# Splitting node rows on two engines: VectorE makes the remainders and third parts, GpSimd only rounds; a small pair of steps in the edge loop goes to ScalarE

## The reference

```python
N, E, IN, H, D, EF = 6250, 100000, 256, 8, 32, 3
x1 = layernorm(x)                                   # rows of 256
h  = (x1 @ W.T).reshape(N, H, D)
alpha = (h[src] * a_src).sum(-1) + (h[dst] * a_dst).sum(-1) \
      + (relu(edge_attr @ edge_W.T + edge_b).reshape(-1, H, D) * h[dst]).sum(-1)
alpha = where(alpha >= 0, alpha, 0.2 * alpha)
ex    = exp(alpha - segment_max(alpha, dst)[dst])   # softmax over the edges of a target
attn  = ex / maximum(segment_sum(ex, dst)[dst], 1e-10)
x = x + segment_sum(h[src] * attn[..., None], dst) + bias
x = x + top2_of_8_experts(layernorm(x))             # LN, 256 -> 1024, gelu, 1024 -> 256
```

## Time and profile before

| what | value |
|---|---|
| median of 3 runs | 2120.4 us (2117.72 to 2121.09) |
| the profiled execution's own time | 2123.07 us |
| its span, first to last instruction | 2121.2 us |
| mean granted TensorE clock | 0.963 |
| busy over the span | PE 91%, DVE 73%, ACT 59%, POOL 59% |
| first stage | up to about 116.5 us of the span |
| edge stage | from there to about 1200 us |

### The profile page before, as it was taken

One profiled execution on the slowest core, in us unless ns is written; L12 is line 12 of the kernel. 1 busy time (PEld: TensorE's weight loads), 2 busy tenths in 40 slices (PEclk: granted clock), 3 DMA queues, 4 the chain that ended last, 5 costly groups with the idle time before them and its releaser, 6 DMA issues. The chain is left out here.

```text
span 2121.2 us, 45176 instructions
## 1 busy us (share of the span) xinstructions
PE 1928.2 (91%) x12492; PEld 1499.8 (71%) x12492; DVE 1542.0 (73%) x3518; ACT 1260.7 (59%) x3557; POOL 1248.5 (59%) x1149
## 2 busy tenths in 40 slices
PE   7559899999999999999999666899999999999997
PEld 5426566666666666666666334899999999999996
DVE  7749899999999999999999887544444444444442
ACT  3438788888888888888888565433333333333332
POOL 5777777777777776666665000355555555555553
PEclk9769999999999999999999877999999999999998
DMA  9355555555555555555444596122222222222221
GB/s 250 108 155 156 153 151 156 156 153 154 152 158 149 148 150 142 150 143 143 141 136 120 208 346 130 48 36 36 41 36 36 40 37 36 38 38 36 38 39 23
DMA packets 161229, 242.11 MB, mean 114 GB/s; under 512 B 36895, under 2 KB 115519, under 8 KB 160866
## 3 DMA queue, kind: packets, MB, share of 16 engines
q0 software_dynamic: 61920, 139.45, 27.6%
q1 hardware_dynamic: 90362, 92.12, 14.7%
q10 hardware_dynamic: 8712, 7.65, 1.1%
HBM read 202.22 MB, written 36.91 MB: 113 GB/s over the span
## 5 line engine op out<-in xcount | busy, mean ns | idle before, releaser
L717 POOL DMA_INDIRECT arena<-h_tab,src x784 | 752.9, 960 | 291.1 <-issue 201.7
L1737 ACT ACTIVATE arena<-psum,arena 128x128 f32<-128x128 f32 x840 | 239.5, 368 | 519.0 <-PE psum L1687 519.0
L919 PE MATMUL psum<-arena 128*128 128x264 f32 x1760 | 475.1, 393 | 1.4 <-DVE arena L1016 1.4
L1687 PEld LDWEIGHTS psum<-arena 128*128 128x128 f32 x3360 | 393.1, 193 | 7.7 <-issue 2.4
L1687 PE MATMUL psum<-arena 128*128 128x128 f32 x3360 | 393.7, 276 | 2.0 <-DVE arena L1759 2.0
L898 PE MATMUL psum<-arena 128*128 128x256 bf16 x2640 | 376.3, 278 | 17.6 <-DVE arena L993 17.5
L1703 PE MATMUL psum<-arena 128*128 x1680 | 379.8, 379 | 0.0
L1649 POOL DMA_INDIRECT out_rows<-arena,src x105 | 212.5, 2024 | 250.4 <-DVE arena L1772 247.5
L919 PEld LDWEIGHTS psum<-arena 128*128 128x128 f32 x1760 | 299.6, 190 | 83.7 <-issue 47.9
L898 PEld LDWEIGHTS psum<-arena 128*128 x2640 | 246.1, 98 | 133.2 <-issue 69.6
L1703 PEld LDWEIGHTS psum<-arena 128*128 128x128 f32 x1680 | 311.1, 190 | 38.0
(11 more groups left out here) (241 smaller groups left out, 1965.2 us busy)
## 6 DMA issues: line engine op xcount, KB each, us to landing
arena<-rel_list SPq DMA_DIRECT2D x110, 256.0 KB
arena<-h_tab,src POOLq DMA_INDIRECT x784
arena<-ea_slots SPq DMA_DIRECT2D x440, 27.0 KB
arena<-in_x SPq DMA_DIRECT2D x12, 896.0 KB, 12.8
arena<-in_W SPq DMA_DIRECT2D x16, 512.0 KB, 8.2
arena<-in_W SPq DMA_DIRECT2D x8, 1024.0 KB, 12.2
h_tab<-arena SPq DMA_DIRECT2D x6, 952.0 KB, 7.9
out_rows<-arena SPq DMA_DIRECT2D x5, 896.0 KB, 12.0
```

What stands on the lines that cost most here:

```text
L717: pool.indirect_dma_start(rows[:, (p % RING * U + k) * TW:(p % RING * U + k + 1) * TW], None, d.h_tab[:, :], bass.IndirectOffsetOnAxis(ap= ...
L919: last = nc.tensor.matmul(ps[:, AGG + a % 2, 0:HS], oh[:, a % OH, k, :], msg[:, a % MSG, k, :], start=(k == 0), stop=(k == U - 1))
L1687: last = nc.tensor.matmul(ps[:, UP + 2 * b + h // 4, h % 4 * P:(h % 4 + 1) * P], w_now[:, b, m, h * P:(h + 1) * P], xT[:, b, m * P:(m + 1) ...
L1737: last = nc.scalar.activation(hT[:, b, h * P:(h + 1) * P], ps[:, UP + 2 * b + half, h % 4 * P:(h % 4 + 1) * P], ACT.Gelu, bias=b1_now[:, b ...
```

## The change

In the first stage GpSimd keeps the two roundings of a group; the two subtractions go to VectorE as `without_first_part` and `last_part`, counted by a new semaphore `left`. VectorE's list gets them at hand-chosen places: three between the statistics of groups 4 and 5, one behind those of group 6, eight among the edge attributes. There is a fourth place for node rows, which lies over the last two lists of `pieces` (edge attributes), so ACT's rounding of attribute list 2 has to wait until group 3 has left that place. `STAGE_OF` says which group uses which place, and ACT waits for group i-4 instead of i-3. The turn of the target list on PE and ACT comes one group later (`REL_AT`).

In the edge stage `fall` is made by ScalarE, with the sign turned (Relu of new minus old maximum, and the exponential of its negative), and `scale` too.

```diff
+STAGE_OF = (1, 2, 0, 3, 1, 2, 0)
@@ prepare
+        late_pieces = c.arena[:, lists.at - 2 * PW:lists.at]
+        c.stage.append(late_pieces[:, 0:GT * TW])
-        REL_AT = 3
+        REL_AT = 4
@@ GpSimd
             for i in range(GROUPS - 1):
                 pool.wait_ge(h_copied, (i + 1) * GT + 2)
                 nc.gpsimd.tensor_copy(first, h).then_inc(cast, 1)
-                pool.wait_ge(cast, 4 * i + 1)
-                nc.gpsimd.tensor_tensor(rest, h, first, ALU.subtract).then_inc(cast, 1)
-                pool.wait_ge(cast, 4 * i + 2)
+                pool.wait_ge(left, 2 * i + 1)
                 nc.gpsimd.tensor_copy(second, rest).then_inc(cast, 1)
-                pool.wait_ge(cast, 4 * i + 3)
-                nc.gpsimd.tensor_tensor(third, rest, second, ALU.subtract).then_inc(cast, 1)
-                pool.wait_ge(cast, 4 * i + 4)
@@ ScalarE, take_h
-                    if i >= 3:
-                        act.wait_ge(rows_stored[i - 3], 32)
-                        act.wait_ge(cast, 4 * (i - 3) + 2)
+                    if i >= 4:
+                        act.wait_ge(rows_stored[i - 4], 32)
+                        act.wait_ge(left, 2 * (i - 4) + 1)
@@ ScalarE, first_part
+                if g == 2:
+                    act.wait_ge(rows_stored[3], 32)
+                    act.wait_ge(left, 7)
@@ VectorE
+            def without_first_part(i):
+                h, rest, first, _, _ = parts_of(c, i)
+                dve.wait_ge(cast, 2 * i + 1)
+                if i:
+                    dve.wait_ge(left, 2 * i)
+                nc.vector.tensor_tensor(rest, h, first, ALU.subtract).then_inc(left, 1)
+
+            def last_part(i):
+                _, rest, _, second, third = parts_of(c, i)
+                dve.wait_ge(cast, 2 * i + 2)
+                dve.wait_ge(left, 2 * i + 1)
+                nc.vector.tensor_tensor(third, rest, second, ALU.subtract).then_inc(left, 1)
...
@@ edges, ScalarE
             def factor(ch):
+                before = c_fwd[:, 1 - ch % 2, 2 * CT - 1:2 * CT]
+                act.wait_ge(chain_scanned, 2 * ch + 2)
...
+                nc.scalar.activation(fall, before, ACT.Relu, bias=c_top[:, 0:1], scale=-1.0).then_inc(fall_made, 1)
                 act.wait_ge(fall_made, ch + 1)
-                nc.scalar.activation(fall, fall, ACT.Exp).then_inc(factor_made, 1)
+                nc.scalar.activation(fall, fall, ACT.Exp, scale=-1.0).then_inc(factor_made, 1)
...
+            def node_scale(ch):
+                act.wait_ge(factored, ch + 1)
+                act.wait_ge(first_kept, 2 * ch + 2)
+                if ch > 1:
+                    act.wait_ge(rescaled, ch - 1)
+                nc.scalar.activation(scale, ps[:, SM, 0:H], ACT.Identity, scale=first[:, ch % 4:ch % 4 + 1], bias=others[:, ch % 4:ch % 4 + 1]).then_inc(scale_made, 1)
@@ edges, VectorE
-                nc.vector.tensor_scalar(fall, before, c_top[:, 0:1], 0.0, ALU.subtract, ALU.min).then_inc(fall_made, 1)
...
-                nc.vector.tensor_scalar(scale, ps[:, SM, 0:H], first[:, ch % 4:ch % 4 + 1], others[:, ch % 4:ch % 4 + 1], ALU.mult, ALU.add).then_inc(scale_made, 1)
```

More of the change, by code:

```diff
@@ L116, in parts_of @@
 def parts_of(c, i):
-    h = c.stage[i % 3].rearrange("p (k h f) -> p k h f", h=H, f=FW)[:, :, :, 1:D + 1]
+    h = c.stage[STAGE_OF[i]].rearrange("p (k h f) -> p k h f", h=H, f=FW)[:, :, :, 1:D + 1]
     rest = c.arena[:, LISTS:LISTS + REST_WORDS].rearrange("p (k h f) -> p k h f", k=GT, h=H)
@@ L145, in prepare @@
          xT_made, xT_copied, h_made, h_copied, zeros_stored, lists_gathered, tiles_gathered, rel_made, turned,
-         turned_back, derived, links_made, ends_same, cut, rests, cast) = semaphores(
+         turned_back, derived, links_made, ends_same, cut, rests, cast, left) = semaphores(
             nc, ctx, "p_consts", "p_zeros", "p_w", "p_small", "p_hi", "p_himade", "p_val", "p_below", "p_counted",
@@ L238, in _ @@
             for i in range(GROUPS - 1):
-                h, rest, first, second, third = parts_of(c, i)
+                h, rest, first, second, _ = parts_of(c, i)
                 pool.wait_ge(h_copied, (i + 1) * GT + 2)
                 nc.gpsimd.tensor_copy(first, h).then_inc(cast, 1)
-                pool.wait_ge(cast, 4 * i + 1)
-                nc.gpsimd.tensor_tensor(rest, h, first, ALU.subtract).then_inc(cast, 1)
-                pool.wait_ge(cast, 4 * i + 2)
+                pool.wait_ge(left, 2 * i + 1)
                 nc.gpsimd.tensor_copy(second, rest).then_inc(cast, 1)
-                pool.wait_ge(cast, 4 * i + 3)
-                nc.gpsimd.tensor_tensor(third, rest, second, ALU.subtract).then_inc(cast, 1)
-                pool.wait_ge(cast, 4 * i + 4)
         @block.sync
@@ L276, in tables @@
                 sp.dma_start(d.h_tab[(i * GT + k0) * P:(i * GT + k1) * P, :].rearrange("(k p) n -> p k n", p=P),
[L277 removed]
+                             c.stage[STAGE_OF[i]][:, k0 * TW:k1 * TW].rearrange("p (k n) -> p k n", k=k1 - k0)).then_inc(rows_stored[i], 16)
             def attributes(g):
@@ L484, in _ @@
             nc.vector.memset(c.stage[0].rearrange("p (n f) -> p n f", f=FW)[:, :, 0], 1.0).then_inc(zeros_made, 1)
+            nc.vector.memset(c.stage[3].rearrange("p (n f) -> p n f", f=FW)[:, :, 0], 1.0).then_inc(zeros_made, 1)
             nc.vector.memset(two_stages.rearrange("p (n f) -> p n f", f=FW)[:, :, 0], 1.0).then_inc(zeros_made, 1)
@@ L607, in _ @@
             group(4)
+            without_first_part(0)
+            last_part(0)
+            without_first_part(1)
             deviations(3)
@@ L615, in _ @@
             split_weights()
-            for g in range(SG):
-                without_first(g)
-                third_part(g)
+            without_first(0)
+            without_first_part(2)
+            third_part(0)
+            last_part(2)
+            without_first_part(3)
+            without_first(1)
+            last_part(3)
+            third_part(1)
+            without_first_part(4)
+            without_first(2)
+            last_part(4)
+            third_part(2)
+            without_first(3)
+            without_first_part(5)
+            third_part(3)
+            last_part(5)
+            dve.wait_ge(left, 2 * (GROUPS - 1))
             dve.wait_ge(ends_same, 3)
@@ L1128, in _ @@
                     shift(ch)
-                for ch in due(t, 8):
-                    node_scale(ch)
                 if t % CS in AHEAD_OF and SELECTED * 2 <= t + AHEAD_OF[t % CS] < SLOTS:
```

18 lines of the change are left out of this document (9 added, 9 removed).

## The result

The changed kernel takes 2094.9 us (median of 4 runs, 2094.0 to 2096.4) against 2120.7 us before (4 runs, 2117.7 to 2128.6): ratio 0.9879, 95% interval 0.9856 to 0.9902. 2097 was forecast. The profiled execution took 2095.04 us, with a span of 2093.2 us, 28.0 us less than before.

What follows compares the result with a forecast made beforehand. First stage bound by GpSimd's splitting; edge stage by gathers until about 400 us, then VectorE and TensorE together. 17.9 + 5.6 = 23.5 us off 2123.07 gives 2099.6, less 2.7 for the median: 2097 us, range 2085 to 2110.

Steps and rivals of the forecast that it cites:

- the term of the edges: Edge stage: two operations leaving VectorE gain 0.14 us in each of 40 chunks, 5.6 us.
- the stage: First stage: subtractions moved to VectorE let the first gather start at 99.6 instead of 117.47, gaining 17.9 us.
- four meetings: First stage: VectorE and GpSimd instructions excluding each other on the shared port, four times 1.7 us.
- ScalarE's new wait ahead of attribute list 2: First stage: waiting until group 3's store landed and it left its place costs nothing, covered by an earlier wait.
- The two long waits: ScalarE, first stage: 7.27 us for a store would go; 18.10 us for the first attribute remainder would end 19.2 earlier.
- All of it goes through: First stage to end: as gathers pace the first 15 chunks, the whole 17.9 us reaches the final time.
- the cut down to 0.14: Edge stage, L1054: of its 0.20 us a chunk only 0.14 pays, ScalarE's side being ready at 413.68, VectorE's at 413.62.
- rival 2: Edge stage: 0.40 us a chunk pays in full because ScalarE's run moves with the faster chunk; 2086 us, chance 0.13.
- The chain as the bound: First stage: handing groups between VectorE and GpSimd bounds it; gain 9 there, 5 in the edges, 2106 us, chance 0.20.
- The edges paying in full: Edge stage: all 0.40 us a chunk taken off VectorE arrives, 16 us; total 2086 us, chance 0.13.
- ScalarE as the bound: Edge stage: ScalarE's added 0.5 us a chunk delays TensorE, up to 28 us lost against 18 gained; 2130, chance 0.05.
- Nothing was swallowed: Denies the rival that late gathers or early chunks no faster than TensorE's start-up swallow the gain; 2118, chance 0.06.

Runs made afterwards that it cites:

- experiment 8: Changed kernel with a small register edit, three row places instead of four, the split kept on two engines; ratio 0.9919 to the kernel before, on a slower chip.
- experiment 7: Changed kernel with a small register edit, both subtractions back on GpSimd, four row places kept; ratio 0.9990 to the kernel before, on a slower chip.
- experiments 1 and 2: 1: changed kernel with wait registers taken modulo 512, 2097.6 us. 2: that kernel with the old edge stage, so the new first stage alone, 2109.7 us.
- experiments 3 and 4: Changed kernel with a small register edit, one operation back on VectorE: 3 the node scale, 2099.4 us; 4 the difference of the maxima, 2106.6 us.

## Why the prediction came out right, and which sizes were off

The forecast of 2097 held, and the order of the steps with it. That it came so near is in part luck: the term of the edges was too small, and other sizes were off the other way.

In the changed kernel's own trace the stage gave 17.7 us (at slot 160; 17.9 were put down) and the edges 10.1 (5.6 were put down), 28 us in all by the spans against 23.5. The 2.7 us by which the median was put below the profiled execution weren't there: its profiled run took 2095.04, its median is 2094.9. By the medians the gain is 25.8 us.

- *First stage, order of events.* Tile 21 was put at 45.8 (measured 45.47), the end of the first attribute wait at 61.9 (60.88), the second at 74 (71.72), the third at 83.5 (81.95), the fourth at 90 (88.76), the last row tile's end at 95.4 (93.59), the store's landing behind it at 3.6 (5.0 in the changed kernel), the first gather at 99.6 (99.37). Two errors of about 2 us cancelled here too. Of four meetings counted at 1.7 us, three showed as third parts of 3.46 us, 1.44 more than without. The working has two slips: its own terms put the first attribute remainder's end at 61.6 at the latest (55.2 + 5.4 + 0.95), not 61.8, and between the first two attribute remainders stand two node remainders and a third part, not one of each. ScalarE's new wait ahead of attribute list 2, put at nothing, took 0.56 us, since the wait ahead of it ended sooner than forecast. The two long waits fell for the reasons given. The stop for a store fell by the fourth place (with three places it is back, 3.40 us in experiment 8). The wait for the attribute remainder fell because VectorE's list no longer meets GpSimd's subtractions; experiment 7 shows that the fourth place does nothing for this one. That VectorE only waits for the end of GpSimd's instruction fits here too: the third part at 39.67 meets the rounding that ends at 41.26 (39.57 + 1.69), and 41.26 + 2.02 = 43.28 is, within 0.15 us, where it ended.
- *First stage, what of it arrives.* 17.9 us were to go through whole. Alone it gave 15.7 us by the trace and 12.6 by the medians, with the first gather 16.9 us earlier. By this run the term was 2 to 5 us too large. "All of it goes through" is nearly right by the slots (18.1 at slot 32, 15.9 at the end), but other traces lose up to 3 us on the way.
- *Edge stage.* 5.6 us were forecast, about 12 measured (experiments 1 and 2). L1054 pays, L1069 pays nothing in the chunks, and ScalarE's new work fits into its slack (experiments 3 and 4), as forecast. Mis-sized was L1054. It was counted at its own 0.20 us and cut to 0.14, since ScalarE's side was to be late by 0.06. VectorE's list got 0.24 us shorter, as the wait for the scan's result went too, and 0.20 to 0.22 of it arrived. So the cut down to 0.14 was wrong, and more so as the new Relu took 0.29 us and not 0.20: by the prediction's own working 0.05 would have been left. The rows of before could have warned of the first: 0.24 us from L1049's start to L1054's, for a scan of 0.21. ScalarE's side is the later one now, as the waits of TensorE show (L993's gone, L866's 4.3 us in 10 times), but its work before L866 would then have to come earlier with the chunk. That is the reason that rival 2 gave, here for L1054 alone; no experiment tested it. The second omission was the drain, 2.3 to 2.8 us, which no term held.
- *Rivals.* The chain as the bound (2106) fell: ScalarE ended at 93.6, not beyond 104. The edges paying in full, 0.40 a chunk, fell with a chunk of 18.74 to 18.76 against 18.96: 0.20 to 0.22. ScalarE as the bound fell: 177 of 200 us busy, and its wait ahead of the copy of the logits still 4.1. Nothing was swallowed.
- *The Trainium skill's rules.* "SBUF — State Buffer" of the Trainium skill (section "Who interferes with whom") agrees with the rows: what ran against GpSimd took 3.46 instead of 2.02 us, and with the rounding elsewhere 2.03. The case of two SBUF inputs, which the prediction names, does not cover the 1024-wide CAST, which has one and took 3.90 instead of 0.69 us. By "ScalarE: Activation LUTs" of the Trainium skill (section "Rules for kernel authors"), about 0.3 us an ACTIVATE: the new Relu took 0.29 us and the node scale 0.34, so the page was nearer than the 0.20 taken from L820. The estimate of 1.6 us for the edges that the prediction made from it was wrong all the same: 0.20 to 0.22 us a chunk arrived, not 0.04.

## What to carry to other kernels

When a small instruction is taken off a busy engine, count from its predecessor's start to its successor's, and take off what that distance will be without it (here 0.38 - 0.14), not the instruction's own duration: the wait for the predecessor's result goes with it. Before an operation is moved to relieve an engine, ask whether a wait for another engine stands behind it; then it is only turned into that wait, as the node scale was. Two engines that shut each other out can cost a third more than themselves: here, splitting the work so that GpSimd makes only short casts ended a wait of ScalarE 20 us sooner. When a last transfer lands late, look at the one issued ahead of it.

## What was not expected of the hardware

The same kernel before took 2122 us on one chip and 2568 to 2582 us on three others. The kernels profiled there have chunks of 26.2 to 26.8 us in place of 18.7 to 19.1, and first gathers within 1 us of the same stage's on the faster chips. There the edge stage stalls for up to 6.1 us at a time with TensorE, VectorE and ScalarE all idle, with DMA engines at 0.37 to 0.38. Why is open. The kernels with the new stage gain there too (ratios 0.988 to 0.992), the edge operations alone little or nothing.

The last row store of 408 KB landed in 3.4 or in 4.9 to 5.0 us in runs of the same first stage. It took 3.4 where the store of 544 KB ahead of it was issued 2.6 us before it, and 4.9 to 5.0 where 1.3 us before it.
